# Second pair: P1's copy and the first relu ahead of T2's rounding, adapter's products ahead of P5; VectorE makes the rest of x22's second chunk

## The reference

```
q_emb = relu(cond @ W3 + b3)                       # one row for a batch
x1    = (64 * x + sum of x over the batch) * q_emb
y     = relu(x1 @ W2 + b2)                         # 512 x 512
base  = y @ W_base + b_base                        # 512 x 512
h     = y @ [W_router | A_s | A_r of 6 experts]    # 128 columns: logits, shared and routed adapters
gates = softmax(logits), the two largest of six kept
out   = x + base + (h weighted by gates) @ [b_base; B_s; B_r]
```

## Time and profile before

| | |
|---|---|
| median of 3 runs | 234.22 us (234.22 to 234.82) |
| the profiled execution | 232.66 us, of it the span of the profile 230.9 us |
| busy over the span | PE 97%, PEld 79%, DVE 74%, ACT 48%, POOL 48% |
| granted TensorE clock | 1.0 (2.4 GHz) in every one of the 40 slices |
| matmuls in the second pair's first half (`mh` 0, with `up(5)`) | 54, from 170.76 to 185.38 us |

### The profile page before, as it was taken

One profiled execution on the slowest core, in us unless ns is written; L12 is line 12 of the kernel. 1 busy time (PEld: TensorE's weight loads), 2 busy tenths in 40 slices (PEclk: granted clock), 3 DMA queues, 4 the chain that ended last, 5 costly groups with the idle time before them and its releaser, 6 DMA issues.

```text
span 230.9 us, 2915 instructions
## 1 busy us (share of the span) xinstructions
PE 224.3 (97%) x982; PEld 183.2 (79%) x982; DVE 171.7 (74%) x319; ACT 110.1 (48%) x230; POOL 111.0 (48%) x103
## 2 busy tenths in 40 slices
PE   7999999999999999999999999999999699999994
PEld 3977888888888888888888878888887488888883
DVE  0685979899979979699825999999982968382334
ACT  3178632544436335797336686435665275431010
POOL 4089334068034875889888220469979800000000
PEclk9999999999999999999999999999999999999999
DMA  6999903604067594004439635010226440002044
GB/s 196 326 236 229 283 9 69 147 3 183 16 158 224 189 261 126 6 0 186 183 72 226 147 139 182 0 30 14 74 91 221 189 182 3 0 13 47 21 171 182
DMA packets 32918, 29.05 MB, mean 126 GB/s; under 512 B 5842, under 2 KB 23318, under 8 KB 32903
## 3 DMA queue, kind: packets, MB, share of 16 engines
q1 hardware_dynamic: 31090, 28.69, 44.1%
q10 hardware_dynamic: 1812, 0.17, 0.6%
HBM read 18.89 MB, written 8.39 MB: 118 GB/s over the span
## 4 chain that ended last, share of the span: by engine, by line
PE 77%; DVE 13%; issue 4%; ACT 3%; POOL 3%; DVEq 0%; POOLq 0%
PE m_ps L1319 59%; PE hT L1319 9%; PE m_ps L1355 5%; DVE xs L1033 3%; DVE x_nat L1013 2%; PE m_ps L1296 2%; DVE xs L1054 2%; ACT y_hi L641 1%; PE m_ps L1309 1%; DVE m_ps L1044 1%; PE m_ps L1347 1%; ACT m_ps L642 1%; DVE vsum_pair L1044 1%; POOL x_lo L552 1%; POOL xs L571 1%
## 5 line engine op out<-in xcount | busy, mean ns | idle before, releaser
L470 POOL TENSOR_TENSOR xs<-xs,qT 128x512 f32<-128x512 f32 x22 | 24.1, 1096 | 46.7 <-DVE xs L887 30.8
L1319 PE MATMUL m_ps<-Wb_hi,y_lo 128*128 128x512 f32 x116 | 45.1, 389 | 0.0
L1319 PE MATMUL m_ps<-Wb_lo,y_hi 128*128 128x512 f32 x116 | 45.1, 389 | 0.0
L1319 PE MATMUL m_ps<-Wb_hi,y_hi 128*128 128x512 f32 x116 | 45.1, 389 | 0.0
L641 ACT ACTIVATE y_hi<-m_ps,condT 128x512 fp32r<-128x512 f32 x30 | 20.8, 692 | 16.8 <-PE m_ps L1319 10.0
L1319 PEld LDWEIGHTS m_ps<-Wb_lo,y_hi 128*128 128x128 f32 x116 | 21.8, 188 | 4.6
L1319 PEld LDWEIGHTS m_ps<-Wb_hi,y_lo 128*128 128x128 f32 x116 | 21.8, 188 | 4.5
L1319 PEld LDWEIGHTS m_ps<-Wb_hi,y_hi 128*128 128x128 f32 x116 | 21.8, 188 | 4.5
L902 DVE TENSOR_TENSOR y_lo<-m_ps,y_hi 128x512 fp32r<-128x512 f32 x30 | 20.2, 678 | 5.4 <-ACT m_ps L642 5.2
L1319 PE MATMUL m_ps<-x_hi,W_hi 128*128 128x512 f32 x61 | 23.7, 389 | 0.0
L1319 PE MATMUL m_ps<-x_hi,W_lo 128*128 128x512 f32 x61 | 23.7, 389 | 0.0
(11 more groups left out here) (188 smaller groups left out, 489.3 us busy)
## 6 DMA issues: line engine op xcount, KB each, us to landing
out_dram<-x_nat SPq DMA_DIRECT2D x32, 256.0 KB, 2.2
x_quart<-in_x_dram SPq DMA_DIRECT2D x28, 256.0 KB, 4.9
x_nat<-in_x_dram SPq DMA_DIRECT2D x7, 1024.0 KB, 5.3
gatesT<-wT SPq DMA_DIRECT2D x24, 48.0 KB
x_nat<-in_x_dram SPq DMA_DIRECT2D x4, 256.0 KB, 3.7
W_f<-in_L_cond_W_dram SPq DMA_DIRECT2D x4, 256.0 KB, 6.4
Wb_f<-in_L_ffn_W_base_dram SPq DMA_DIRECT2D x1, 1024.0 KB, 8.9
W_sb<-in_L_cond_W_dram SPq DMA_DIRECT2D x2, 256.0 KB, 4.9
```

The source lines that it names most:

```text
L470: return nc.gpsimd.tensor_tensor(per_batch(tile), per_batch(tile), qT[:, c, BG * g:BG * (g + 1)].unsqueeze(2).to_broadcast([P, BG, N]), AL ...
L1319: mm = nc.tensor.matmul(psum, lhsT, rhs, start=start and i == 0, stop=stop and i == len(terms) - 1)
```

## The change

- In both pairs ScalarE rounds x22,1 earlier: in the first after T1,1 of the same pair, in the second ahead of T1,1. `OPERANDS` becomes one order for each pair.
- In both pairs VectorE instead of GpSimd makes the rest of x22,1 (`x22_rest`, a new semaphore `x22_lo_ready`): in the first pair after its last chunk of preparation and before `C11(0)`, in the second after `add_x(4, 3)` and before `C11(0)`. GpSimd's `rest("x22", 1)` goes, which stood in front of T4,1.
- In the second pair ScalarE copies P1 and makes `relu_pair(0, 0)` before it rounds T2,1.
- In the second pair VectorE makes `y_rest_pair(0, 0)` before `add_x(5, 0)`.
- In the second pair TensorE's `up(5)` stands ahead of P5.

```diff
-        OPERANDS = (("x11", 0), ..., ("x21", 1), ("T1", 1), ("T2", 1), ("T3", 1), ("x22", 1), ("T4", 1))
+        OPERANDS = ((("x11", 0), ("T1", 0), ("x22", 0), ("T2", 0), ("T3", 0), ("x21", 0), ("T4", 0),
+                     ("x11", 1), ("x21", 1), ("T1", 1), ("x22", 1), ("T2", 1), ("T3", 1), ("T4", 1)),
+                    (("x11", 0), ("T1", 0), ("x22", 0), ("T2", 0), ("T3", 0), ("x21", 0), ("T4", 0),
+                     ("x11", 1), ("x21", 1), ("x22", 1), ("T1", 1), ("T2", 1), ("T3", 1), ("T4", 1)))
...
+        def wait_rest(eng, p, name, kk):
+            if (name, kk) == ("x22", 1):
+                eng.wait_ge(x22_lo_ready, p + 1)
+            else:
+                by_pool = [operand for operand in OPERANDS[p] if operand != ("x22", 1)]
+                eng.wait_ge(pair_lo_ready, len(by_pool) * p + by_pool.index((name, kk)) + 1)
...
 # GpSimd, prepare(p)
                 rest("T2", 1)
                 rest("T3", 1)
-                rest("x22", 1)
                 T4(1)
                 rest("T4", 1)
...
 # ScalarE
             operand(0, "T1", 1)
+            operand(0, "x22", 1)
...
-                operand(p, "T2", 1)
-                copy_p1(0)
+                if p == 0:
+                    operand(p, "T2", 1)
+                    copy_p1(0)
+                else:
+                    copy_p1(0)
+                    relu_pair(0, 0)
+                    operand(p, "T2", 1)
                 operand(p, "T3", 1)
-                operand(p, "x22", 1)
                 if p == 0:
                     hw_split(g - 1)
-                relu_pair(0, 0)
+                    relu_pair(0, 0)
                 operand(p, "T4", 1)
...
+                operand_next("x22", 1)
                 operand_next("T1", 1)
...
 # VectorE
+            def x22_rest(p):
+                dve.wait_ge(pair_hi_ready, nth_operand(p, "x22", 1))
+                nc.vector.tensor_tensor(lo_of("x22", 1), tile_of("x22", 1), hi_of("x22", 1).bitcast(F32),
+                                        ALU.subtract).then_inc(x22_lo_ready, 1)
...
             whole_pair(0, 7)
+            x22_rest(0)
...
                     C11(0)
-                    add_x(g - 1, 0)
                     y_rest_pair(0, 0)
-                    add_x(g - 1, 1, 2, 3)
+                    add_x(g - 1, 0, 1, 2, 3)
                     u_2(0)
...
                 add_x(g, 3)
+                if more:
+                    x22_rest(p + 1)
...
 # TensorE, second pair
                     pe.wait_ge(hw_lo_ready, g)
+                    up(g - 1, 0, 1, 2, 3)
                     blocks(0, 5)
-                    up(g - 1, 0, 1, 2, 3)
                     pe.wait_ge(out_ready, TT * (g - 2) + TT)
                     blocks(0, 6)
```

More of the change, by code:

```diff
@@ L187, in adaln_ffn @@
         q64_ready, pool_offset_ready, offset_ready, act_full_ready = sem("q64_ready"), sem("pool_offset_ready"), sem("offset_ready"), sem("act_full_ready")
-        combo_ready, pair_hi_ready, pair_lo_ready = sem("combo_ready"), sem("pair_hi_ready"), sem("pair_lo_ready")
+        combo_ready, pair_hi_ready, pair_lo_ready, x22_lo_ready = sem("combo_ready"), sem("pair_hi_ready"), sem("pair_lo_ready"), sem("x22_lo_ready")
         product_done, p1_copied, adds_ready, gates_last_ready, last_spread = sem("product_done"), sem("p1_copied"), sem("adds_ready"), sem("gates_last_ready"), sem("last_spread")
@@ L220, in adaln_ffn @@
         BY_SCALAR = (((0, 0), (1, 2), (0, 1)), ((0, 0), (0, 1), (1, 1)))
-        OPERANDS = (("x11", 0), ("T1", 0), ("x22", 0), ("T2", 0), ("T3", 0), ("x21", 0), ("T4", 0),
-                    ("x11", 1), ("x21", 1), ("T1", 1), ("T2", 1), ("T3", 1), ("x22", 1), ("T4", 1))
+        OPERANDS = ((("x11", 0), ("T1", 0), ("x22", 0), ("T2", 0), ("T3", 0), ("x21", 0), ("T4", 0),
[3 rows of a table added]
         COMBOS = (("T1", 0), ("T2", 0), ("T3", 0), ("T4", 0), ("T1", 1), ("T2", 1), ("T3", 1), ("T4", 1))
@@ L239, in nth_operand @@
         def nth_operand(p, name, kk):
-            return len(OPERANDS) * p + OPERANDS.index((name, kk)) + 1
+            return len(OPERANDS[0]) * p + OPERANDS[p].index((name, kk)) + 1
+        def wait_rest(eng, p, name, kk):
[4 more added lines that the diff above has]
+                eng.wait_ge(pair_lo_ready, len(by_pool) * p + by_pool.index((name, kk)) + 1)
         def nth_combo(p, name, kk):
@@ L1029, in turn_pair @@
                 if p > 0:
-                    dve.wait_ge(pair_lo_ready, nth_operand(p - 1, "T4", c % 2))
+                    wait_rest(dve, p - 1, "T4", c % 2)
                 elif half == 1:
@@ L1502, in blocks @@
                         if mh == 0:
-                            pe.wait_ge(pair_lo_ready, nth_operand(p, operand, kk))
+                            wait_rest(pe, p, operand, kk)
                         mm = product(ps, [(W_hi[:, k0 + kk, cols], lo_of(operand, kk))], False, kk == 1)
```

## The result

The changed kernel takes 230.75 us (median of 4 runs, 230.42 to 230.83), the kernel before 234.22 (4 runs, 234.10 to 234.82): ratio 0.9844, 95% interval 0.9825 to 0.9863. The forecast was 232.2, with a range of 231.5 to 233.3. It named the right sign and too small a gain: 3.5 us where it said 2.0. Yet the two profiled executions differ by 232.66 - 230.42 = 2.24 us only. The profile is as forecast, and the medians are not; most of what follows is about that difference.

A forecast was written before the change was run, and what follows sets the result against it. TensorE was taken to set the end, losing 2.38 us in the second pair's window, mostly before P3. Second pair -2.13 plus first pair +0.15 gave about -2.0 us: median 234.22 to 232.2, range 231.5 to 233.3.

The forecast's parts named there:

- The second pair: Window from its first product to its other half's: of 2.38 us lost by TensorE, 0.25 stay, so -2.13 us.
- P3's stall: Second pair: TensorE's 2.11 us wait for `u2` before P3 goes, with 0.4 us of slack.
- T4,1's rest 0.13 late for P4: Second pair: GpSimd's rest ends 0.13 us behind P4's last matmul's need; a matmul that waited loses another 0.09 to 0.11.
- The first pair: VectorE's rest of x22,1 meets GpSimd at work and delays T2,1's rest: +0.15 us, bounds 0 and 0.5.
- its 1.56 above the profiled one: In the sum: the median's 1.56 us above the profiled execution stays, so profiled 230.7 gives median 232.2.
- GpSimd first in the second pair: Rival: GpSimd starts T1,1's rest before VectorE's x22,1 rest, C11 1.45 us late; about 233.0; 0.14 together with stall-moves rival.
- the stall only moves to P4: Rival: T4,1's rest isn't earlier, P4 loses 1.3 us, gain near 1.0, 233.2; 0.14 together with GpSimd-first rival.
- Starving in the first pair: Rival: VectorE gets its second input only when GpSimd pauses, C11 3.7 us late, TensorE stalls 3.2 us; 235.3, chance 0.05.
- giving back later: Rival: group 6's gates arrive late through their DMA and give the 2 us back; 234.2, chance 0.05.

The follow-up runs named there:

- e11: Changed kernel with VectorE's order, TensorE's order and the first pair's x22,1 move undone together; 230.36 us, ratio to before 0.9873.
- e4: Kernel before, plus eight matmuls leading nowhere ahead of the second pair's P7, filling the wait in front of P3; 232.88 us, ratio 0.9972.
- e3: Changed kernel with GpSimd again making x22,1's rest in its old place in the first pair only; 230.60 us, ratio to before 0.9899.
- e5: Changed kernel in which the second pair's P3 also waits for T4,1's rest, putting a long wait back; 234.57 us, ratio to before 1.0036.
- e1_orders: Kernel before with only the second pair's three new orders (ScalarE, VectorE, TensorE), x22,1's rest left on GpSimd; 231.66 us, ratio 0.9935.
- e2: Changed kernel with all three second-pair orders undone, leaving only x22,1's earlier rounding and rest on VectorE; 232.18 us, ratio to before 0.9953.
- e8: Changed kernel with ScalarE's second-pair order undone, P1's copy again behind T2,1's rounding; 232.96 us, ratio to before 0.9996.
- e0_before: Kernel before, unedited, run again for a second profile; ratio 1.0003, profiled execution 233.86 us.

## Why the prediction was wrong

**The steps in the profile held.** The second pair: forecast -2.13, measured 12.49 - 14.62 = -2.13. P3's stall gone with slack, T4,1's rest 0.13 late for P4 and 0.25 lost with what follows: both as forecast. The first pair: forecast +0.15; P1 to P1 is 51.99 instead of 51.84, so +0.15. But that agreement is partly luck: among the kernels in which VectorE doesn't meet GpSimd there, P1 to P1 goes from 51.74 to 52.24, and among those in which it does from 51.96 to 52.24 as well. In e11 and e4 a wait of 0.2 to 0.3 us near 130 us, before P4 of the first pair, is about as large, and comes and goes with the execution. Undoing the collision (e3) made TensorE's matmul there punctual and didn't show in the time (230.60 beside 230.50, on another chip; ratios 0.9899 and 0.9880). What is left of 2.24 us, 0.27, lies in the first 45 us, whose length varies by 0.8 us from one execution to another in these profiles (the same matmul stands at 44.94 to 45.70).

**The step that failed** is in the sum: "the median 234.22 to 232.2; its 1.56 above the profiled one stays as it is". It doesn't stay. It was the price of the same stall, paid in the executions that were timed and not in the one profiled: behind the wait in front of P3 TensorE runs at 1.2 GHz for some 3 us in about half of the executions (44 of 86 by their clocks). That costs 1.6 us in the profile that caught it, and 1.36 between the medians of the groups. The prediction priced the stall at its length alone, 2.11 us, and put this term at nothing. The gain is thus 2.2 us against one half of before's executions (232.73 - 230.50) and 3.6 against the other (234.09 - 230.50). By their times of 234.10 to 234.82, as their clocks are not on record, the four executions of the first measurement were all of the slower half, and the profiled one of 232.66 was of the faster. That draw was luck; against the median of all 86 executions, 233.6, the gain is 3.1. The e4 run shows that it is the wait, as filling it with work that leads nowhere took the upper group away with the schedule as it was; the e5 run shows that a wait alone is enough.

The warning stood in the numbers: three runs at 234.22, 234.22 and 234.82, and a profiled one 1.56 us (0.7%) below all of them, when the three spread by 0.26%. I took that as an offset. The profile couldn't show the reason, since its clock is 1.0 in all 40 slices, but the wait of 2.11 us was the only long idle stretch of TensorE behind the start, and a case "the clock falls behind it in the timed executions", 1.56 us, belonged among the rivals. It would have given 234.22 - 1.98 - 1.56 = 230.7.

**The rivals.** GpSimd first in the second pair: no, VectorE's rest of x22,1 ran from 172.55 in its usual 0.68 us, and GpSimd's next began 0.6 us after it, at 173.14. That the stall only moves to P4: not here, but e1_orders is that case, with 1.23 us of waits in P4 and 231.66. Starving in the first pair and giving back later: neither.

**What each part is worth.** ScalarE's order takes the wait in front of P3 away (without it 232.96). The second pair's rest on VectorE takes 1.2 us out of P4 (e1 to the changed kernel). Alone it is worth more than forecast (e2, 232.18), by a roundabout way: ScalarE's rounding no longer stands before the first relu, the wait shrinks to 1.7 us, and none of twelve executions is in the upper group.

**What stays open.** How the chance of a fallen clock depends on the wait: none of 12 at 1.7 us (e2), 44 of 86 at 2.1, two of ten at some 2.5 (e8), eight of twelve at 2.7 (e5). The chance doesn't simply grow with the wait, the samples are small and of different chips, and why one execution keeps its clock and the next does not isn't shown.

## What to carry to other kernels

When the profiled execution is faster than every timed one by more than they spread, don't carry the difference over: profile the kernel again until one from the slower end is caught, and look at the pitch of the matmuls behind each long wait. A stall of TensorE is priced at its length plus what the clock may cost behind it, here 2.1 and up to 1.6 us; where the stall can't be removed, matmuls that lead nowhere can fill it. And an in-order queue is read for what stands between two short operations of one chain: here one rounding in front of a copy cost 3 us of chain, and another between copy and relu 0.4.

## What the runs showed of the hardware that was not expected

A wait of 2.1 us of a TensorE that had been busy for over 100 us brings its clock to 1.2 GHz in about half of the executions (44 of 86 by their mean clocks), for about 3.4 us in each of the three profiles that show it, beginning 1 us after the wait's end in one profile (e0_before, from 183.2), 0.8 to 0.9 us after it in another (e5_hold_long) and before its end in a third (e8_copy_back, where a window over the wait has 0.98 and the one behind it 0.50). In the changed kernel's first pair a VectorE instruction with two SBUF inputs, begun 0.67 us before a GpSimd instruction on SBUF was over, took 0.54 us longer than alone and left that one's 1.29 us as they were; the next GpSimd instruction, begun 0.59 us before VectorE's was over, took 0.46 us longer.
